# Masked attention in two stages: VectorE adds the mask in the pass that finds the score's extreme, and the exponentials run in place in SBUF

## What is computed

```python
def _causal_attn(q, k, v):                      # second layer, called twice, head size 16
    scale = 1.0 / math.sqrt(q.shape[-1])
    scores = jnp.einsum('bthd,bshd->bhts', q, k) * scale
    mask = jnp.tril(jnp.ones((t, t), dtype=bool))
    attn = jax.nn.softmax(jnp.where(mask, scores, -jnp.inf), axis=-1)
    return jnp.einsum('bhts,bshd->bthd', attn, v)

def local_attention(q, k, v):                   # third layer, six times, head size 64
    ...                                         # keys i-64 .. i of query i
    mask = (it < jb) | (it > jb + w) | (jb == -1)
    sim = jnp.einsum('bhwie,bhwje->bhwij', bq, bk2) * QK_SCALE
    attn = jax.nn.softmax(jnp.where(mask, sim, -jnp.finfo(sim.dtype).max), -1)
    out = jnp.einsum('bhwij,bhwje->bhwie', attn, bv2)
```

## Time and profile before

| | us |
|---|---|
| median of three runs | 4542.27 |
| lowest and highest run | 4541.48, 4546.44 |
| span of the profiled execution, first to last instruction | 4533.8 |
| what lies around the span, against the median | 8.5 |

### The profile page before, as it was taken

How to read it: one execution, slowest core, us unless ns; L and a number is a source line. 1 busy time by engine, 2 the same in 40 slices (tenths; PEclk the granted TensorE clock), 3 DMA queues, 4 the chain that set the end, 5 groups by cost and what they waited for, 6 DMA issues and landing times. The chain is left out here.

```text
span 4533.8 us, 83813 instructions
## 1 busy us (share of the span) xinstructions
PE 4131.4 (91%) x30832; PEld 2952.2 (65%) x30832; DVE 3154.7 (70%) x7414; ACT 2854.8 (63%) x5769; POOL 1819.9 (40%) x1862
## 2 busy tenths in 40 slices
PE   6999999988988999999999999977999999986898
PEld 4555555555757788887888878864555555544787
DVE  5677777776777667666676676645677777767645
ACT  3666666667866776767767777733666666664322
POOL 3222222213557555555555555523222222201544
PEclk8999999999999999999999999998999999998999
DMA  6655655535020001011010111017556655522265
GB/s 152 137 108 101 111 99 110 95 62 209 1 75 5 26 21 44 15 38 33 27 33 14 37 33 34 16 37 141 118 103 113 113 107 109 91 45 69 79 177 187
DMA packets 208206, 354.18 MB, mean 78 GB/s; under 512 B 26927, under 2 KB 110564, under 8 KB 205745
## 3 DMA queue, kind: packets, MB, share of 16 engines
q1 hardware_dynamic: 200217, 338.42, 33.5%
q0 software_dynamic: 7584, 10.39, 0.7%
HBM read 257.48 MB, written 114.98 MB: 82 GB/s over the span
## 5 line engine op out<-in xcount | busy, mean ns | idle before, releaser
L757 DVE TENSOR_REDUCE xa_m_part<-xa_ring 128x1 f32<-128x512 f32 x2048 | 1319.2, 686 | 503.5 <-PE xa_ring L910 489.0
L679 ACT ACTIVATE xa_ex<-xa_sc 128x1024 f32<-128x1024 f32 x1024 | 991.6, 1022 | 124.4 <-PE xa_sc L896 109.7
L910 PE MATMUL xa_ring<-xa_ks,xa_q_base 48*128 48x512 f32 x2048 | 521.5, 500 | 169.7 <-DVE xa_m_part L757 130.1
L1077 POOL TENSOR_SCALAR lt_p<-lt_p,lt_stat 128x192 f32<-128x192 f32 x384 | 360.4, 939 | 507.4 <-DVE lt_stat L1067 507.1
L924 PE MATMUL xa_pv<-xa_ex,xa_vs 128*17 128x256 f32 x8192 | 553.4, 388 | 1.1 <-issue 1.1
L910 PEld LDWEIGHTS xa_ring<-xa_ks,xa_q_base 48*128 48x128 f32 x2048 | 202.7, 186 | 500.4 <-DVE xa_m_part L757 431.8
L1090 ACT ACTIVATE lt_p<-lt_bank,lt_stat,lt_rq 128x128 f32<-128x128 f32 (+1 forms) x768 | 365.7, 480 | 218.9 <-DVE lt_stat L1060 214.5
L1929 PE MATMUL lt_bank<-lt_wp,lt_xt 128*128 128x512 f32 x1728 | 461.9, 409 | 16.0 <-DVE lt_wp L1766 7.1
L896 PE MATMUL xa_sc<-xa_q_base,xa_ks 50*128 50x256 f32 x4096 | 424.5, 303 | 27.7 <-ACT xa_k L659 4.1
L896 PEld LDWEIGHTS xa_sc<-xa_q_base,xa_ks 50*128 50x128 f32 x4096 | 349.4, 189 | 121.2 <-ACT xa_vs L666 24.4
L1929 PEld LDWEIGHTS lt_bank<-lt_wp,lt_xt 128*128 128x128 f32 x1728 | 314.6, 192 | 79.3 <-DVE lt_xt L1759 8.4
(11 more groups left out here) (332 smaller groups left out, 8166.4 us busy)
## 6 DMA issues: line engine op xcount, KB each, us to landing
xa_ks<-keys SPq DMA_DIRECT2D x372, 256.0 KB
keys<-xa_kp SPq DMA_DIRECT2D x128, 512.0 KB, 3.8
xa_cx<-in_ctx_t SPq DMA_DIRECT2D x64, 512.0 KB
lt_u<-in_lt_wqkv SPq DMA_DIRECT2D x54, 256.0 KB
places<-in_moe_blank SPq DMA_DIRECT2D x47, 258.0 KB, 8.7
moe_xs<-places SPq DMA_DIRECT2D x47, 258.0 KB
lt_w<-in_lt_w SPq DMA_DIRECT2D x6, 1536.0 KB
xa_q_base<-xa_m_rows SPq DMA_DIRECT2D x512, 2.0 KB
```

Source lines behind the costliest of these rows:

```text
L679: act.activation(x.ex[:, n % x.NE, :, :], x.sc[n % 2][:, :, :], ACT.Exp).then_inc(*x.ex_done.one())
L757: dve.tensor_reduce(x.m_part[:, i % 2, qt, h, ch:ch + 1], x.bank(n + odd), AX.X, ALU.max).then_inc(*x.dve_out.one())
L910: pe.matmul(x.bank(n + odd), x.q_base[rows, pair, b * S + qt * P:b * S + (qt + 1) * P], x.ks[unit % x.NU][rows, pair % 4, ch * 512:(ch + 1 ...
L1077: pool.tensor_scalar(sv, sv, self.stat[:, n % 5, 3, 1:2], None, ALU.mult).then_inc(*self.div_pool.one())
```

## The change

VectorE now makes one fused pass for each query tile: it reads the bare scores from PSUM and the mask from SBUF, writes (score + mask) * (-scale) to `p` and leaves the smallest of these in `stat`. ScalarE then computes exp(-p + smallest) in place in `p`. So the mask's product, the bfloat16 mask and identity with their casts, and the small bias instruction are gone. A score bank is free once VectorE has read it. In Local the factor 8 over the norm is stored with a minus sign.

```diff
@@ Attention.pe_step, front
-            on.wait_ge(self.exp_done, 2 * (n - NS) + 2)
-            pe.matmul(s[:, 0:self.width], self.c.ident_bf[:, :], st.mask[:, :], start=True, stop=False)
+            on.wait_ge(self.low_done, 2 * (n - NS) + 2)
             for q in range(2):
                 mm = pe.matmul(s[:, self.off[q]:self.off[q] + self.keys[q]], st.q_of(b, h, q),
-                               st.k_of(b, h, self.first[q], self.keys[q]), start=False, stop=(q == 1))
+                               st.k_of(b, h, self.first[q], self.keys[q]), start=True, stop=True)
@@ Attention.dve_step, front
             on.wait_ge(self.s_full, n + 1)
-            on.wait_ge(self.div_dve, 2 * (n - 5) + 2)
-            on.wait_ge(self.div_pool, n - 4)
+            on.wait_ge(self.t_full, n - 4)
             for q in range(2):
-                dve.tensor_reduce(t3[:, 0, q:q + 1], s[:, self.off[q]:self.off[q] + self.keys[q]], AX.X,
-                                  ALU.max).then_inc(*self.max_done.one())
-            on.wait_ge(self.max_done, 3 * n + 2)
-            if st.scale is None:
-                dve.scalar_tensor_tensor(t3[:, 1, :], t3[:, 0, :], -1.0, st.scale_of(b, h, slice(0, 2)),
-                                         ALU.mult, ALU.mult).then_inc(*self.max_done.one())
-            else:
-                dve.tensor_scalar(t3[:, 1, :], t3[:, 0, :], -st.scale, None,
-                                  ALU.mult).then_inc(*self.max_done.one())
+                at = slice(self.off[q], self.off[q] + self.keys[q])
+                to = slice(self.place[q], self.place[q] + self.keys[q])
+                dve.tensor_tensor_reduce(self.p[:, n % 5, to], s[:, at], st.mask[:, at], st.minus_scale(b, h, q),
+                                         -NEG, ALU.add, ALU.min,
+                                         t3[:, 0, q:q + 1]).then_inc(*self.low_done.one())
@@ Attention.act_step, front
-            s = self.s_banks[n % len(self.s_banks)]
-            on.wait_ge(self.max_done, 3 * n + 3)
-            on.wait_ge(self.t_full, n - 4)
             for q in range(2):
-                at = slice(self.off[q], self.off[q] + self.keys[q])
-                to = slice(self.place[q], self.place[q] + self.keys[q])
-                act.activation(self.p[:, n % 5, to], s[:, at], ACT.Exp, bias=t3[:, 1, q:q + 1],
-                               scale=st.scale_of(b, h, slice(q, q + 1)) if st.scale is None else st.scale,
+                low = self.p[:, n % 5, self.place[q]:self.place[q] + self.keys[q]]
+                on.wait_ge(self.low_done, 2 * n + q + 1)
+                act.activation(low, low, ACT.Exp, bias=t3[:, 0, q:q + 1], scale=-1.0,
                                accum_out=t3[:, 2, q:q + 1]).then_inc(*self.exp_done.one())
@@ Conv (Local likewise: load_mask, the step "mask", rq, scale_of)
-            self.mask = sb("mask", [P, 3 * P], BF16)
+            self.mask = sb("mask", [P, 3 * P])
...
+    def minus_scale(self, b, h, q):
+        return -1.0 / float(np.sqrt(self.DH))
...
-        sp.dma_start(self.at.p[:, 0, 0:3 * P], g("causal")).then_inc(*self.mask_in.one())
+        sp.dma_start(self.mask[:, :], g("causal")).then_inc(*self.mask_in.one())
...
-        dve.tensor_copy(self.mask[:, :], self.at.p[:, 0, 0:3 * P]).then_inc(*self.mask_ready.one())
-        on.wait_ge(self.mask_ready, 1)
@@ Local
-                    pool.tensor_scalar(self.rq[:, j % 2, tile, :], n[:, 2, :], 8.0, None,
+                    pool.tensor_scalar(self.rq[:, j % 2, tile, :], n[:, 2, :], -8.0, None,
...
-    def scale_of(self, j, h, q):
-        return self.rq[:, j % 2, q, h]
+    def minus_scale(self, j, h, q):
+        return self.rq[:, j % 2, q, h:h + 1]
@@ Load.finish
-        on.wait_ge(self.ident_loaded, 1)
-        dve.tensor_copy(c.ident_bf[:, :], c.ident[:, :])
```

More of the change, by code:

```diff
@@ L8 @@
 F32 = mybir.dt.float32
-BF16 = mybir.dt.bfloat16
 F32R = mybir.dt.float32r
@@ L987, in __init__ @@
         f = c.flow
-        self.s_full, self.max_done, self.exp_done = f("at_s_full"), f("at_max_done"), f("at_exp_done")
+        self.s_full, self.low_done, self.exp_done = f("at_s_full"), f("at_low_done"), f("at_exp_done")
         self.div_dve, self.div_pool = f("at_div_dve"), f("at_div_pool")
@@ L1136, in __init__ @@
                                 self.STRIPS, GH // self.STRIPS, 0)
-        self.scale = 1.0 / float(np.sqrt(self.DH))
         f, d = c.flow, c.dma_flow
         self.w_in, self.cw_in, self.mask_in = d("w_in"), d("in0"), d("mask_in")
-        self.zero_pool, self.zero_act, self.mask_ready = f("ca_zero_pool"), f("ca_zero_act"), f("mask_ready")
+        self.zero_pool, self.zero_act = f("ca_zero_pool"), f("ca_zero_act")
         self.normed, self.turned, self.rest = f("normed"), f("turned"), f("half")
@@ L1383 @@
     HP = H // 2
-    scale = None
     TICKS, HEADS, FEATURES, LOW, ROLL = 24, 24.18, 16.45, 17.33, 61.35
@@ L1419, in __init__ @@
             self.ffc, self.lnc = sb("ffc", [P, DEPTH, 2, FC]), sb("lnc", [P, DEPTH, 2, KC])
-            self.mask = sb("mask", [P, 3 * P - WINDOW], BF16)
+            self.mask = sb("mask", [P, 3 * P - WINDOW])
             self.next, self.xt = sb("next", [P, S]), sb("xt", [P, 2, 2, KC, S], F32R)
@@ L1434, in __init__ @@
         self.park_out, self.park_in, self.small_in = d("out0"), d("out1"), d("small_in")
-        self.mask_in, self.mask_ready = d("mask_in"), f("mask_ready")
+        self.mask_in = d("mask_in")
         self.scl_in, self.b2_in = d("in15"), d("in16")
@@ L1605, in sp @@
             elif kind == "load_mask":
-                sp.dma_start(self.at.p[:, 0, 0:3 * P - WINDOW], g("band")).then_inc(*self.mask_in.one())
+                sp.dma_start(self.mask[:, :], g("band")).then_inc(*self.mask_in.one())
             elif kind == "fs":
@@ L1749, in dve @@
                 on.wait_ge(self.mask_in, 1)
-                dve.tensor_copy(self.mask[:, :],
-                                self.at.p[:, 0, 0:3 * P - WINDOW]).then_inc(*self.mask_ready.one())
-                on.wait_ge(self.mask_ready, 1)
                 dve.memset(self.at.p[:, :, P:P + WINDOW], 0.0).then_inc(*self.p_zero.one())
@@ L3094, in build @@
         c.minus_half = sb("minus_half", [P, 64])
-        c.ident, c.ident_bf = sb("ident", [P, P]), sb("ident_bf", [P, P], BF16)
+        c.ident = sb("ident", [P, P])
         c.stats, c.mean_var = sb("stats", [P, NT, 6]), sb("mean_var", [P, NT, 2])
```

## The result

| us | before | after |
|---|---|---|
| median of the runs side by side | 4541.88 (4540.15 to 4546.44, 4 runs) | 4471.5 (4462.04 to 4472.37, 4 runs) |
| span of the profiled execution | 4533.8 | 4469.0 |
| Local, first front to last score product on TensorE | 1614.6 | 1562.3 |
| Conv, first pass and second pass | 89.4, 90.5 | 80.8, 79.7 |

The ratio is 0.9838, with a 95% interval of 0.9825 to 0.9851: 70 us faster. Between the two profiled executions Local gives 52.3 us and Conv's two passes 19.4 us, 71.7 together; their spans differ by only 64.8, so the other stages were 7 us longer in the second.

A forecast was written before the change was run, and what follows sets the result against it. The prediction took TensorE to bound Local, and Conv with ScalarE close behind. Its terms, 52 + 7 - 17 + 10 + 1 = 53 us, taken from 4542.3 gave 4489, with a range of 4460 to 4530.

The forecast's parts named there:

- the first case: Whole kernel: the forecast itself, a gain of 35 to 80 us (4462 to 4507); chance 0.65.
- TensorE's slot, 52 us: Local, TensorE's queue: dropping the mask's product returns its whole slot, 384 x 0.135 = 52 us.
- The wait for a bank, +7 us: Local's fronts on TensorE: VectorE's pass frees the score bank earlier, saving 7 us, at most 14.
- The give-back, -17 us: Local, TensorE's waits for VectorE: they grow and return a third of the 52 us; bounds 0 and 52.
- VectorE, +12 ns a head: Local, VectorE: fused passes and accumulator reads less the small step add 12 ns a head, 5 us over 384 heads.
- ScalarE in Local, nothing: Local, ScalarE: exponentials 69 ns shorter, 53 us less work, and starting sooner, yet costed at nothing.
- Conv, 10 us: Conv: a head falls from 1.41 to 1.33 us, 128 x 0.08 = 10 us; bounds 18 us gain, 10 us loss.
- Small things, 1 us: First fronts of both stages: no wait for casts and copies of mask and identity, 1 us together.
- The 8.5 us around the span: Whole kernel: the runs' median lies 8.5 us above the profiled span, and this is carried over.
- the second: Rival, Local: VectorE's lateness returns some 35 of the 52 us, gain 20 us, 4522; chance 0.16.
- The third: Rival, VectorE's queue: fused pass at half rate, a third of 222 us shows in Local, 58 us slower, 4600; chance 0.11.
- The fifth: Rival, Local and Conv: no wait comes back, Conv reaches ScalarE's floor, gain 85 us, 4457; chance 0.04.

The follow-up runs named there:

- e2: Kernel after the change with a bfloat16 product of zeros put back in front of the scores: Local 1603.1 us, ratio 0.9959 to the kernel before.
- e1: Kernel before the change with only the mask's product left out, scores unmasked: Local 1583.9 us, ratio 0.9906 to the kernel before.
- e3: Kernel after the change with a score bank freed by the exponentials again, not VectorE's pass: Local 1561.0 us, ratio 0.9848 to the kernel before.
- e12: Kernel after, small 128x2 step back, exponentials waiting for it, written as a reduction over a one-element axis: Local 1574.1 us, ratio 0.9888 to the kernel before.
- e9: Kernel after, two-input 128x2 step put back between fused passes and exponentials, which wait for it: Local 1587.8 us, ratio 0.9926 to the kernel before.
- e8: Kernel after, Local's exponential reading its scale of -1 for each partition from SBUF: Local 1562.9 us, ratio 0.9826 to the kernel before.
- e11: Kernel after with the step of e9, but exponentials wait only for their own fused passes: Local 1582.9 us, ratio 0.9893 to the kernel before.
- e7: Kernel after, a head's first exponential waiting for both fused passes: Local 1562.8 us, Conv passes 83.6 and 84.3, ratio 0.9876 to the kernel before.
- e5: Kernel after with three spare 128-column reductions on VectorE behind each head's fused passes: Local 1596.5 us, ratio 1.0006 to the kernel before.

## Why the prediction was right, and where its terms were wrong

It forecast 4489 with a range of 4460 to 4530; the median is 4471.5. The direction, the stages and TensorE as Local's bound were right, and the gain of 70 us lies inside the first case's 35 to 80. The sum was 53. Its first term was right in size; the bank was counted too high, VectorE's part and Conv too low.

- **TensorE's slot, 52 us: right as a slot.** 52.9 by the starts in the trace, 53.3 for e2's product. The three transposes without a gap were a fair reason that no weight load hid there. That Local gained 52.3 is in part luck: 31 or 41 us of the slot arrive, by e1 and e2, and the shorter chain brings the rest.
- **The wait for a bank, +7 us: nothing in the new chain**, by e3. I took the waits of the old chain for what the earlier freed bank would save; with the new chain 3.0 us of them are left even when the exponential frees the bank.
- **The give-back, -17 us: about right, but another term was missing.** 22 us of the slot come back as waits with the old chain, 12 with the new. "These waits must grow" did not come true: the two largest rows have 27.6 us where they had 27.1, because the shorter chain took 11.5 to 21.6 us of waits away. The prediction has no term for that: it took VectorE as unchanged and put the earlier start of the exponentials at nothing.
- **VectorE, +12 ns a head: mis-sized by adding up rows.** The passes' rows are as forecast: 410 ns for 192 columns (0.41), 291 for 128 (0.29), and the companion 81 ns (83). But the companions start together with the next instruction and take no place of their own, and the small step stood until the reductions' rows had ended (1803.60 + 0.54 = 1804.14), to be followed by the reciprocal after 79 ns (median). An ordinary head before and after:

```profile
1803.60 0.54 DVE L1056 TENSOR_REDUCE lt_stat<-lt_bank 128x1 f32<-128x128 f32 x2
1804.18 0.16 DVE L1060 SCALAR_TENSOR_TENSOR lt_stat<-lt_stat,lt_rq 128x2 f32<-128x2 f32 x1
1804.25 0.16 DVE L1067 RECIPROCAL lt_stat<-lt_stat 128x2 f32<-128x2 f32 x1
1804.45 0.29 DVE L1070 TENSOR_SCALAR lt_p<-lt_p,lt_stat 128x128 f32<-128x128 f32 x1
```

```profile
1865.85 0.34 DVE L1053 CUSTOM_DVE_ANT_0 lt_p<-lt_bank,lt_mask,lt_rq 128x128 f32<-128x128 f32 x1
1866.11 0.08 DVE L1053 DVE_READ_ACCUMULATOR2_ANT lt_stat<- 128x1 f32 x1
1866.11 0.41 DVE L1053 CUSTOM_DVE_ANT_0 lt_p<-lt_bank,lt_mask,lt_rq 128x192 f32<-128x192 f32 x1
1866.45 0.08 DVE L1053 DVE_READ_ACCUMULATOR2_ANT lt_stat<- 128x1 f32 x1
1866.45 0.16 DVE L1058 RECIPROCAL lt_stat<-lt_stat 128x2 f32<-128x2 f32 x1
1866.65 0.29 DVE L1061 TENSOR_SCALAR lt_p<-lt_p,lt_stat 128x128 f32<-128x128 f32 x1
```

  From first start to last end VectorE needs 55 ns less at an ordinary head and 318 ns less at the 64. The mean of 282 ns for L1060 hid these: 161 ns at most heads and some 0.89 us at 64 ((384 x 282 - 320 x 161) / 64), which lie between the rotation of queries and keys and their norms, for which TensorE's turn waits. e12 shows the hold as a cause for the step of e9. For the old L1060 equal rows suggest the same, but it is not run by itself, so that this is what the shorter chain saves is argued and not shown.
- **ScalarE in Local, nothing: right for its shorter work**, by e8. The exponential lost 58 ns, not 69. Its earlier start is not nothing: with the small step back, the exponentials' wait for it costs 1587.8 - 1582.9 = 4.9 us (e9 against e11).
- **Conv, 10 us: 19.4.** The prediction's 1.27 us of ScalarE's work a head is what was found (77.84 / 79.00 of a head), and its exponential got 30 to 34 ns longer where I took 19. But the steady head takes 5.147 / 4 = 1.29 us, not 1.33: "three engines within 15% of one another do not run without waits" was not borne out, with ScalarE at 98.5%. And it took 5.755 / 4 = 1.44 us before, not the 1.41 that I had read over the whole pass. By e1 the product brought 10.9 of the gain. The other 8.5 come from the chain: e7 shows 7.2 us for letting ScalarE start after the first pass, e9 against e11 9.8 us for a wait on a small step; these two overlap, since that step waits for both passes.
- **Small things, 1 us**: too small to be seen.
- **The 8.5 us around the span** did not stay: after the change the median lies 2.5 us above the profiled span, and each execution 1.8 us or so above its own. The profiled execution before was probably shorter than the median; its time is not on record.

Slot and Conv alone, 52 + 19 = 71, come to the 70.4 measured; this hides a give-back and a shorter chain of about one size, and 7 us in other stages that the spans of the two profiled executions differ by.

On the Trainium skill ("VectorE: DVE Perf Modes", section on the TRN2 errata), whose fixed cycles gave an estimated 43 ns more for an exponential from SBUF: the trace lies between, 30 and 34 ns. Its floor of 1.32 us a head was not borne out, 1.29 was measured. The Trainium skill's rule of halved throughput ("Vector Engine (DVE) Microarchitecture Reference", section on points easy to get wrong) does not touch a pass with one input in PSUM: 1.00 ns a column. An accumulating pass with both inputs in SBUF was not tried.

Of the rivals, the second charged 35 us of the 52 as given back; e1 measures 22 with the old chain, e2 12 with the new. The third, slower, needed a fused pass at half rate, which did not occur; that its third of VectorE's added time was too much is shown only for work that nobody waits for, in e5. The fifth, "better than the forecast", 85 us, named what came out, no net give-back in Local and ScalarE's floor in Conv, but counted 14 us for the bank.

Of what the profile was to show, Conv's fronts (82 to 85 us forecast, 80.8 and 79.7 found) and Local (1568 to 1585, 1562.3 found) were both too long, and TensorE's waits for VectorE did not grow.

## What to carry to other kernels

Before a small instruction is priced by its mean, look at its shortest, median and longest: where the mean is far above the median, something holds it at a few places, and these may be the places that matter. Price it by the starts around it and not by its row: on VectorE too the rows overlap. Taking work off the bound and shortening the chain behind it are not two separate gains: here 31 and 12 us alone, 52 together. So a gain that equals the slot taken out does not show that nothing was given back; it took both halves to see it. And an extreme that goes straight from the pass that found it to the exponential saves the step, its wait and the wait of the second pass for the first, which counts where ScalarE is nearly full, as in Conv; in Local the wait of the second pass cost nothing (e7).

## What was not expected of the hardware

- VectorE's pass with an accumulator runs at the rate of a plain one: 291 ns for 128 and 419 ns for 256 columns, PSUM and SBUF in, fp32. Reading the accumulator is 81 to 83 ns and its row starts before the pass's row ends (1577.76 above, where the pass ends at 1577.42 + 0.41 = 1577.83).
- A copy of 128x2 in SBUF takes 160 ns with two inputs and 170 with one, and up to 980 ns beside GpSimd's 128x512 product of two SBUF tensors; as a reduction it takes 155 ns and was never held. Beside GpSimd's scaling of `p` the two-input copy took 160 to 163 ns.
- A scale for each partition costs ScalarE 91 to 93 ns an exponential (e8), where the prediction took 88.
